# A mixture-of-experts loop on one core: a scratch write and a wait behind every gather and scatter that Pool issues

## The reference, cut to what matters

```python
x = x + _layernorm(attn_ref(_layernorm(x), ...))      # Nystroem attention, a graph term: not touched here
x = x + _layernorm(ffn_ref(_layernorm(x), ...))
def ffn_ref(x, keys, w1, b1, w2, b2, rw, rb):         # E = 16 experts, TOP_K = 4, F = 512, D = 128
    logits = -dist2(x, keys) + x @ rw.T + rb
    topv, topi = jax.lax.top_k(logits, TOP_K)
    w = jax.nn.softmax(topv, axis=-1)
    hidden = gelu(x @ w1.T + b1)                      # per expert
    exp_out = hidden @ w2.T + b2                      # per expert
    return sum over the 4 chosen experts of w * exp_out
```

## Time and profile before

| | |
|---|---|
| median of 3 runs | 646.68 us |
| span of the profiled execution | 694.4 us |
| time of the profiled execution beyond its span | not given by the page |
| PE busy | 536.4 us (77%) |
| DVE busy | 364.9 us (53%) |
| ACT busy | 353.7 us (51%) |
| POOL busy | 281.1 us (40%) |
| gathers (L592) | 128, mean 980 ns |
| scatters (L600) | 128, mean 1002 ns |
| mean granted clock of TensorE | 0.923 |
| expert loop, first gather to last scatter | 229.6 to 664.6 us |

### The profile page before, as it was taken

One profiled execution on the slowest core, in us unless ns is written; L12 is line 12 of the kernel. 1 busy time (PEld: TensorE's weight loads), 2 busy tenths in 40 slices (PEclk: granted clock), 3 DMA queues, 4 the chain that ended last, 5 costly groups with the idle time before them and its releaser, 6 DMA issues.

```text
span 694.4 us, 19926 instructions
## 1 busy us (share of the span) xinstructions
PE 536.4 (77%) x6242; PEld 481.6 (69%) x6242; DVE 364.9 (53%) x1325; ACT 353.7 (51%) x1079; POOL 281.1 (40%) x308
## 2 busy tenths in 40 slices
PE   4999879994502789977678789789977776679984
PEld 4967779993401489976677679678967776668942
DVE  6554779997999356545434553112334432233126
ACT  6524167775556365546445667336634434335513
POOL 4000000000451543566666743664566666645520
PEclk9999999998655799999999999999999989989998
DMA  8970000006001455444444645445866644546553
GB/s 229 255 280 9 3 3 0 0 0 243 1 1 76 120 161 157 138 131 131 131 140 143 204 124 162 135 144 146 264 207 180 183 130 133 145 122 192 174 197 122
DMA packets 55746, 92.28 MB, mean 133 GB/s; under 512 B 10352, under 2 KB 26096, under 8 KB 55152
## 3 DMA queue, kind: packets, MB, share of 16 engines
q1 hardware_dynamic: 45424, 72.35, 35.0%
q0 software_dynamic: 10240, 18.89, 9.2%
HBM read 78.07 MB, written 17.37 MB: 137 GB/s over the span
## 4 chain that ended last, share of the span: by engine, by line
PE 43%; issue 18%; DVE 18%; POOL 8%; ACT 7%; DMA 2%; DVEq 2%; another core or an unknown queue 0%; POOLq 0%; SPq 0%; ACTq 0%
PE bank L2148 15%; PE bank L2141 13%; POOL yd L600 6%; ACT value L883 3%; DVE shared L1187 2%; DVE shared L1179 2%; POOL shared L592 2%; DVE early L1467 2%; PE bank L1735 2%; DMA shared<-yd 1%; PE bank L1772 1%; PE bank L1840 1%; PE bank L1762 1%; PE bank L2133 1%; PE bank L2089 1%
## 5 line engine op out<-in xcount | busy, mean ns | idle before, releaser
L883 ACT ACTIVATE value<-bank,shared 128x128 f32<-128x128 f32 x632 | 180.8, 376 | 203.0 <-PE bank L2141 156.7
L2148 PE MATMUL bank<-shared,value 128*128 x1264 | 182.7, 290 | 62.4 <-ACT value L883 41.7
L2148 PEld LDWEIGHTS bank<-shared,value 128*128 128x128 f32 x1264 | 161.7, 200 | 76.7 <-issue 76.1
L2141 PE MATMUL bank<-early,shared 128*128 x1264 | 180.9, 288 | 5.3 <-issue 2.8
L592 POOL DMA_INDIRECT shared<-xd,early x128 | 125.5, 980 | 127.5 <-PE bank L2141 79.8
L2141 PEld LDWEIGHTS bank<-early,shared 128*128 128x128 f32 x1264 | 162.6, 200 | 9.3 <-issue 8.4
L1663 DVE SCALAR_TENSOR_TENSOR early<-bank,value,early 128x128 f32 x158 | 55.4, 351 | 195.8 <-PE bank L2148 116.6
L600 POOL DMA_INDIRECT yd<-early x128 | 128.3, 1002 | 67.8 <-DVE early L1663 36.2
L560 POOL TENSOR_TENSOR shared<-shared,xn 128x512 f32<-128x512 f32 x4 | 5.1, 1264 | 174.9 <-DVE xn L1262 167.1
L2133 PE MATMUL bank<-ident,shared 128*128 128x128 f32 x128 | 35.9, 284 | 9.0 <-DMA shared<-xd,early 5.7
L2003 PE MATMUL bank<-ksp,shared 128*128 128x32 bf16 x1536 | 40.9, 177 | 0.0
(11 more groups left out here) (334 smaller groups left out, 689.3 us busy)
## 6 DMA issues: line engine op xcount, KB each, us to landing
shared<-w1b SPq DMA_DIRECT2D x158, 258.0 KB
w1b<-in_w_t SPq DMA_DIRECT2D x1, 4096.0 KB, 17.8
shared<-col_dram SPq DMA_DIRECT2D x1, 4096.0 KB, 13.4
shared<-in_w_t SPq DMA_DIRECT2D x1, 4096.0 KB, 12.3
att<-yd SPq DMA_DIRECT2D x8, 512.0 KB
shared<-yd SPq DMA_DIRECT2D x4, 1024.0 KB, 9.1
xd<-xnT SPq DMA_DIRECT2D x2, 1280.0 KB
shared<-xd,early POOLq DMA_INDIRECT x128
```

Source lines behind the costliest of these rows:

```text
L883: ins = act.activation(hT[:, i % 2, tok(c)], bank[2 + i % 2][:, tok(c)], ACT.Gelu, bias=w1_now[:, i % WR, F + c:F + c + 1])
L2141: ins = mm(bank[2 + i % 2][:, tok(c)], w1_now[:, i % WR, tok(c)], x_now, start=True, stop=True)
L2148: ins = mm(bank[6 + i % 2][:, 0:D], hT[:, i % 2, tok(c)], w2_sb[:, bass.ds(e, 1), c, :] .rearrange("p a d -> p (a d)"), start=(c == 0), st ...
```

## The change

Pool gets a scratch tile of 128 partitions by 64 f32 columns and a semaphore. A function `pause` writes zeros into the tile, which raises the semaphore, and Pool waits for it. It is called behind the issue of each of the 128 gathers and 128 scatters. The tile is read by nobody.

```diff
+        pause_to = sb("pause_to", [P, P // 2])
...
+        paused = sem("paused")
...
+            pauses = [0]
+
+            def pause():
+                pool.memset(pause_to[:, :], 0.0).then_inc(paused, 1)
+                pauses[0] += 1
+                pool.wait_ge(paused, pauses[0])
+
             def rows(n):
...
                 pool.indirect_dma_start(out=xg[:, n % XR, :], out_offset=None, in_=xd[n // JT][:, :],
                                         in_offset=bass.IndirectOffsetOnAxis(ap=idx_src[:, n:n + 1], axis=0))\
                     .then_inc(xg_in[n % XSEM], 16)
+                pause()
 
             def results(m):
...
                                         in_=yg[:, m % SLOTS, :], in_offset=None).then_inc(y_out[m % RING], 16)
+                pause()
```

## The result

The changed kernel takes 672.69 us (median of 4 runs, 669.0 to 675.83) where the kernel before takes 646.76 (643.97 to 647.09) in the runs beside it: ratio 1.043, 95% interval 1.0375 to 1.0486. That is 25.9 us slower. The forecast was 688.7, with a range of 655 to 718.

The account below looks back on a forecast made before the run. Pool was taken to bound the plain pair stretches at 2.56 us a tile. Long pair stretches 37.0, middle 3.25 and start 1.75 sum to 42.0 us, added to 646.7 for 688.7; range 655 to 718.

Parts of the forecast that it names:

- What bounds the kernel: In the long pair stretches Pool's own gather and scatter time, 2.56 us a tile, was taken as the plain bound.
- the 47.7 us put down to recording: Recorded span of 694.4 us against the plain median of 646.7; late releases there were taken to belong to the recording.
- 40 of 47.7: Pair stretches and middle: recording's cost if plain pairs take 2.56 us, 35.5 + 5 = 40 us of the excess span.
- One pause: Behind each gather or scatter: memset and wait add 0.25 us to Pool, from 0.15 to 0.45.
- The long pair stretches: 74 pairs of gather and scatter: 74 x 2 x 0.25 = 37.0 us, all on the path; a pair becomes 3.06.
- The middle and the start: 13 middle pairs, half the pauses counted: 3.25 us; seven pauses before the eighth gather at the start: 1.75 us.
- Gathers alone, scatters alone, the tail: Stretches of only gathers or only scatters: pauses fit in idle time and add nothing; tail scatters stay 1.79 us apart.
- A shared port: Pair stretches: VectorE's L1523 could lock Pool's memsets out, up to 11 us by the skill's rule; counted as nothing.
- Cover: Rival, 12%: late releases happen in plain runs too, and 0.48 us idle a pair takes up the pauses; 653 us.
- the pauses let TensorE's news through: Rival, 5%: pauses break back-to-back runs of Pool's DMAs, ending late releases; pairs of 3.00 us, faster at 641 us.
- The cold start: Rival, 3%: every change from memset to DMA costs 0.78 us, a pause 1.03; about +180 us, 827.
- vanish in the gap: Rival, 2%: the pause does nothing, hidden in the 0.30 us gap between Pool's DMAs; 647 us.

Follow-up runs that it names:

- the doses: Against the kernel before: pauses waited for later 649.15 us, pauses writing 8 columns 662.79, the changed kernel 672.69, two pauses behind each DMA 773.31.
- the second recording of the kernel before: The kernel before, unchanged, recorded once more: 700.42 us, span 698.7, beside 699.1 for its plain runs.

## Why the prediction was right, and where not

**What bounds the kernel.** Right for the times it was made for, with one leg of the argument false. Pool's own time as the bound of the pair stretches is borne out by the doses. The time added to a start-to-start was 0.04, 0.105, 0.155 and 0.72 us, and the kernels became 8.2, 21.8, 25.9 and 132 us slower; 148 times the dose is 6, 16, 23 and 107. Already the smallest costs its share (8.2 us, 5 to 12 by its interval), so the kernel before has no idle time there that takes up pauses when prompt. It is shown from the side only: no prompt recording of the kernel before exists. The false leg is the 47.7 us put down to recording. They were the late condition, which is real in plain runs, and a span is 1.7 us below its own execution's time. The sum that seemed to confirm it (40 of 47.7) set prompt times against a late recording and hit because both numbers were right, not the reason. (It also counts 14 tiles in the middle where the stretch holds 13 intervals: the pace there was 3.03 us, not 2.94.) It was luck that the changed kernel was timed in a prompt set. In the late one the same change costs 12.5 us and the forecast of 42 would have been far off, for a reason that the prediction had weighed only as a rival. That the recorder presses back on the engines, which the Trainium skill (NOTIFIC — the notification-queue block, section 7.1) led me to lean on, is shown by nothing here.

**One pause.** This is the term that was mis-sized, and with it the forecast difference of 42.0 us: 0.25 forecast, 0.155 measured in the pair stretches, 1.39 - 1.25 = 0.14 at the start. It lay at the lower end. The memset (0.15 priced, 0.17 measured) and what follows it up to the DMA (0.28 priced, 0.27 measured) were right in themselves. What I put in beside them was a gap of 0.09 between DMA and memset and a little for a second wait instruction; the memset starts at the DMA's end and the DMA 0.27 after the memset. The changed kernel's start shows it:

```profile
233.75 0.96 POOL L601 DMA_INDIRECT shared<-xd,early  x1 [0.28 <-POOL pause_to L590]
234.70 0.17 POOL L590 MEMSET pause_to<- 128x64 f32 x1
235.14 0.95 POOL L601 DMA_INDIRECT shared<-xd,early  x1 [0.27 <-POOL pause_to L590]
```

The same sum with 0.155 is 148 x 0.155 + 26 x 0.155/2 + 7 x 0.155 = 22.9 + 2.0 + 1.1 = 26.0 us, and 25.9 were measured. That it comes so close is partly luck: the middle alone came to 4.8 us by the recordings, not 2.0, and the runs of one kernel spread by 3 to 10 us.

**The long pair stretches.** Right: most of the loss is there (3.76% of 4.3%), all of it on the path. A pair was to take 3.06, it took 2.87 on Pool's timeline and 2.93 to 2.94 on average.

**The middle and the start.** 5.0 us forecast for both. The pauses outside the long stretches cost 5.3 us when tried alone in the late condition. In the prompt one the middle has 4.8 us.

**Gathers alone, scatters alone, the tail.** Right in the main: 1.96 us a tile, with 1.91 in the kernel that has pauses in the long pair stretches alone, and 1.79 us a scatter once Pool has caught up. The prediction took the tail as evenly spaced from its start, from one row. Its first 15 scatters leave no idle time for a pause (1.42 us apart, 1.27 in that other kernel), but they delay the end little: from the last gather to the last scatter pass 44.6 us, and 43.4 there.

**A shared port.** Neither the memsets' median of 0.166 us nor the pace leaves room for the 11 us by the rule of the Trainium skill (SBUF — State Buffer, Practical consequences). (Only 7 of the 16 instructions from 590.8 on lie in the pair stretch, so the prediction's count was too high as well.) The recording of the changed kernel has such an instruction (L1523 before, L1534 here) beside a memset by chance:

```profile
603.78 0.34 DVE L1534 TENSOR_SCALAR xn<-xn,rstd,nmr 128x128 f32<-128x128 f32 x1
603.83 0.17 POOL L590 MEMSET pause_to<- 128x64 f32 x1
```

As recorded, the memset lies wholly inside VectorE's instruction and both keep their usual length; so it is at 609.8 and 611.6. The trace does not tell whether VectorE ran these in its 2-port mode, and no run here set a memset against such an instruction by design.

**The rivals.** Cover is wrong in the prompt condition and half right in the late one, where 148 x 0.155 = 23 us of pauses cost 12.5. Its premise, that late releases happen in plain runs too, was true. That the pauses let TensorE's news through is refuted: they were set beside late releases, and those stayed. The cold start did not occur: a DMA behind a memset keeps its 0.96 us. Nor did the pause vanish in the gap.

## What to carry to other kernels

Where one engine issues two kinds of DMA in turn, add up their start-to-start times for a tile before looking at its busy share: Pool was 40% busy over the span and still the bound for 74 of 128 tiles. A wait that Pool makes for its own last instruction cost more here than the instruction (0.115 us and 0.04 of the 0.155); wait as late as the data allow. And ask whether a recording is of the same condition as the times beside it: span and time of one execution differ here by 1.7 us, so a gap of 48 is a finding, not an overhead.

## What the hardware showed that I had not expected

A second write and wait in a row costs far more than the first. With one pause a DMA starts 0.27 us after the memset ends, with two 0.61 to 0.64, though the second memset itself starts 0.22 us after the first. Fitting, but not shown: Pool's queue prepares the next DMA behind one unmet wait but not behind two.

A queued memset hides most of itself: 0.17 us long, it costs 0.04 between two DMAs.

There is a late condition, in which engines hear of TensorE late when Pool runs its DMAs back to back: up to 5 us in the kernel before, over 8 with `NEAR = 12`. It holds for a whole set of runs and adds 51 to 60 us to the kernel before (641 to 647 against 697 to 701); the same chip showed both. It moved with Pool's activity: with half of the scatters 58.5 us went, and with gathers sent further ahead the gather-only stretch slowed from 2.06 to 2.37 us a tile. The news comes once Pool has stopped: of the 45 late activations in the second recording of the kernel before, 43 start in an idle stretch of Pool over 0.5 us long, typically 1.0 us after its last DMA ended. Pool waits for the same news there, so this alone doesn't tell cause from effect. What makes a set late, and what holds the news back, stays open.
